# Attention edge gathers of a graph network: lanes without an edge get an index past the table and are left unfetched

## The reference, cut to what matters

```
xn = layernorm(x)
k, q, v = typed_matmul(xn, W, node_type)              # [n, 4 heads, 64]
q_att = einsum('nhd,rhde->rnhe', q, relation_att)     # 8 relations
v_msg = einsum('nhd,rhde->rnhe', v, relation_msg)
score = sum(q_att[etype, dst] * k[src], -1) * relation_pri[etype] / 8
alpha = softmax of score over the edges of one dst
agg   = segment_sum(alpha * v_msg[etype, src], dst)
```

## Time and profile before

| what | us |
|---|---|
| median of three executions | 8423.68 |
| profiled execution | 8421.28 |
| its span | 8419.7 |
| attention stage, first L996 to last L996 | 908.3 to 3488.3 |
| busy in the whole span: TensorE, VectorE, ScalarE, GpSimd | 5151.1, 4515.7, 3197.1, 3888.6 |
| HBM traffic | 878.85 MB read, 280.36 MB written |

### The profile page before, as it was taken

One profiled execution on the slowest core, in us unless ns is written; L12 is line 12 of the kernel. 1 busy time (PEld: TensorE's weight loads), 2 busy tenths in 40 slices (PEclk: granted clock), 3 DMA queues, 4 the chain that ended last, 5 costly groups with the idle time before them and its releaser, 6 DMA issues. The chain is left out here.

```text
span 8419.7 us, 105906 instructions
## 1 busy us (share of the span) xinstructions
PE 5151.1 (61%) x30143; PEld 3822.5 (45%) x30143; DVE 4515.7 (54%) x8736; ACT 3197.1 (38%) x7600; POOL 3888.6 (46%) x3841
## 2 busy tenths in 40 slices
PE   2999566666666666564823333333333257699999
PEld 2555355554555545343712222221222146588888
DVE  5555577777777777634423333343333499833333
ACT  0554466666666666412300100000101067543333
POOL 1221566666666666451267667667776423100000
PEclk7999899999999999886856666655555589799999
DMA  6554777777777777642222222233333468700000
GB/s 142 203 211 191 216 212 214 212 215 213 215 215 210 214 212 213 162 143 93 88 69 66 68 61 66 65 81 83 82 83 82 88 223 287 232 19 12 12 12 12
DMA packets 540060, 1157.67 MB, mean 137 GB/s; under 512 B 121739, under 2 KB 273458, under 8 KB 532798
## 3 DMA queue, kind: packets, MB, share of 16 engines
q0 software_dynamic: 217216, 691.51, 29.0%
q1 hardware_dynamic: 299864, 438.79, 16.2%
q10 hardware_dynamic: 22480, 21.44, 0.8%
HBM read 878.85 MB, written 280.36 MB: 138 GB/s over the span
## 5 line engine op out<-in xcount | busy, mean ns | idle before, releaser
L954 POOL DMA_INDIRECT ae_kv<-edge_table,ae_index x1664 | 1604.5, 964 | 1028.4 <-issue 833.9
L2220 POOL DMA_INDIRECT g_row<-y_parts,g_index x1664 | 1699.1, 1021 | 739.9 <-issue 658.3
L1172 PE MATMUL psum<-ae_kv,ae_edge_hot 128*128 128x266 f32 x3328 | 897.5, 416 | 543.1 <-ACT ae_step_sums L1062 212.7
L1172 PEld LDWEIGHTS psum<-ae_kv,ae_edge_hot 128*128 128x128 f32 x3328 | 629.5, 199 | 797.2 <-issue 407.8
L2241 PE MATMUL psum<-g_row,g_keep 128*128 128x64 bf16 x4992 | 345.4, 216 | 904.0 <-issue 837.1
L1141 PE MATMUL psum<-ae_q,ae_node_hot 128*128 x3328 | 800.8, 395 | 66.2 <-DMA ae_q<-queries 50.0
L996 DVE TENSOR_TENSOR ae_kv<-ae_kv,psum 128x2048 f32<-128x2048 f32 x208 | 475.6, 2287 | 529.2 <-remote 491.0
L2241 PEld LDWEIGHTS psum<-g_row,g_keep 128*128 128x128 bf16 x4992 | 258.7, 113 | 1004.3 <-issue 947.2
L1141 PEld LDWEIGHTS psum<-ae_q,ae_node_hot 128*128 128x128 f32 x3328 | 634.8, 196 | 170.5 <-issue 84.5
L3131 ACT ACTIVATE em_h<-psum,experts_affine 128x256 f32<-128x256 f32 (+1 forms) x800 | 404.4, 555 | 611.7 <-PE psum L3088 432.4
L2414 DVE TENSOR_TENSOR g_acc<-g_acc,g_step_sums 128x64 f32 x832 | 188.3, 226 | 815.8 <-issue 427.1
(11 more groups left out here) (593 smaller groups left out, 10321.5 us busy)
## 6 DMA issues: line engine op xcount, KB each, us to landing
ae_node_hot<-rel_rows SPq DMA_DIRECT2D x208, 512.0 KB
edge_hots<-g_keep SPq DMA_DIRECT2D x208, 356.0 KB
gn_hots<-edge_hots SPq DMA_DIRECT2D x208, 356.0 KB
gn_row<-source_places SPq DMA_DIRECT2D x208, 256.0 KB
ae_kv<-edge_table,ae_index POOLq DMA_INDIRECT x1664
g_row<-y_parts,g_index POOLq DMA_INDIRECT x1664
pair_sums<-gn_out SPq DMA_DIRECT2D x624, 4.0 KB
x_sorted<-nt_x SPq DMA_DIRECT2D x52, 128.0 KB
```

Source lines behind the costliest of these rows:

```text
L954: g.indirect_dma_start(out=kv[:, s, n, :], out_offset=None, in_=dram["table"], in_offset=bass.IndirectOffsetOnAxis(ap=index[:, s, n:n + 1] ...
L1172: ins = t.matmul(bank[4 + m % 2][:, 0:CW], ohs[:, n, :], kv[:, s, n, KC:2 * D], start=n % 2 == 0, stop=n % 2 == 1)
L2220: g.indirect_dma_start(out=row[:, m, n, :], out_offset=None, in_=table, in_offset=bass.IndirectOffsetOnAxis(ap=index[:, m, n:n + 1].bitcas ...
```

## The change

In the index stage VectorE makes a tile `far`: 0 where the destination is below N and inside the block, and FAR = 1,048,576 elsewhere. It sets the first lane of every step and all lanes of the first 64 steps back to 0 and adds `far` to the row of table indices. So an index is either a real one (0 to 49,999) or over a million. In the attention stage each gather takes a bound, R*N - 1 = 49,999, past which a lane is not fetched and no error is raised; that lane keeps what its slot held.

```diff
+        far = sbt("far", [P, RB, P])
...
+            ch.link(v.scalar_tensor_tensor(far[:], st[:, :, 0, :], float(N), inb[:], ALU.is_lt, ALU.mult))
+            ch.link(v.tensor_scalar(far[:], far[:], -float(FAR), float(FAR), ALU.mult, ALU.add))
+            ch.link(v.memset(far[:, :, 0:1], 0.0))
+            ch.link(v.memset(far[0:64, 0, :], 0.0))
+            ch.settle()
+            ch.done(v.tensor_tensor(st[:, :, 2, :], st[:, :, 2, :], far[:], ALU.add))
...
-                                     in_offset=bass.IndirectOffsetOnAxis(ap=index[:, s, n:n + 1].bitcast(U32), axis=0)
-                                     ).then_inc(gathered[s], 16)
+                                     in_offset=bass.IndirectOffsetOnAxis(ap=index[:, s, n:n + 1].bitcast(U32), axis=0),
+                                     bounds_check=R * N - 1, oob_is_err=False).then_inc(gathered[s], 16)
```

## The result

| comparison | before, us | changed, us | ratio, 95% interval |
|---|---|---|---|
| first measurement | 8418.60 (8401.67 to 8434.99) | 8442.72 (8421.99 to 8455.14) | 1.0024 [1.0013, 1.0034] |
| a second one | 8417.21 | 8431.45 (8418.64 to 8442.12) | 1.0018 [1.0009, 1.0027] |
| a third, on another chip | 7728.35 (7726.48 to 7732.76) | 7779.37 (7770.87 to 7785.61) | 1.0063 [1.0049, 1.0077] |

The change makes the kernel slower: by 24 and 14 us where the kernel before takes 8420 us, and by 51 us on a chip where it takes 7728. That one unchanged program takes 9% longer on one chip than on another was not foreseen, and it turned out to decide what the change costs.

A forecast was written before the change was run, and what follows sets the result against it. The prediction took a chain of VectorE and TensorE waits, not gathers, as the bound. 8421.28 + 5.2 (index stage) + 0 (bound) - 1 (lanes left out) = 8425.5 us profiled, median 8428, range 8405 to 8446; likeliest no telling difference, 73%.

The forecast's parts named there:

- Index stage: Five added VectorE instructions ahead of `inblock`, covered by nothing: 5.2 us more, between 4.95 and 6.0.
- So 0.01 to 0.04 us more for each; I take 0.04: Attention stage: extra time the bound adds to each of 1664 gathers, sized from bounded scatters; 0.32 us a group.
- Covered by the 2.46 us that GpSimd waits. Cost 0: Attention stage: the bound's 0.32 us a group hides in GpSimd's wait; cover gone at 0.28 us more a gather.
- L996's idle total down by 50 us or more (the gathers paced it): Profile sign that the forecast is wrong: VectorE's wait before L996 shrinks from 529 us, the gathers having paced it.
- I take -1: Attention stage: 12,891 unfetched lanes, 26.4 MB, shorten nothing on the chain; gain 1 us, bounds 0 and -44.
- VectorE's 9.4 us, then TensorE's 2.8 us: Attention stage: the chain that sets the 12.25 us turn, with the gathers lying beside it.
- The gathers do pace the stage: Rival, attention stage: L996 waits for gathered data, so less traffic gives 8303 to 8357, say 8340 us; 6%.
- Relief of the other transfers: Rival, attention stage: irregular turns come from traffic and give back half of their 44 us: 8407 us; 8%.
- The bounded gather is slow, and GpSimd becomes the bound: Rival, attention stage: from 0.28 us more a gather GpSimd's issues set the turn; at 0.45, 8705 us; 7%.
- The lanes are fetched all the same: Rival, attention-stage gathers: left-out lanes are still fetched or cost as much; 8429 us; 4%.
- A gather reports its end late or not at all: Rival, attention stage: a gather with lanes left out leaves VectorE waiting for `gathered`; under 1%.
- shift by turn-length pattern: Attention stage: a small delay changes how often other turn lengths occur, shifting 20 or more us either way; 4%.

The follow-up runs named there:

- index work only: The changed kernel with `far` all zero and no bound on the gathers: 8421.77 us, ratio 1.0007 to the kernel before.
- bound only: The kernel before with only the bound added to L954's gathers: 8440.38 us, ratio 1.0029; on a quick chip 7791.32 us, ratio 1.0082.
- nothing left out: The changed kernel with `far` all zero, index work and bound kept: 8443.47 us, ratio 1.0034 to the kernel before.
- first-lane run: The changed kernel with `far` at FAR everywhere, so past the first 64 steps each gather fetches one row: 7795.16 us against 7734.87, ratio 1.0077.

## Why the prediction was right, and where it was not

The time, 8442.72, lies in the range, 3 us from its upper end, but the case called likeliest, no difference that can be told, did not come: +24 us (0.24%) is slightly more than that bound. Part of the hit is luck. The sum has 0 for the bound, which alone costs 23 us, and -1 for the lanes left out, which give back about 12; the two errors have opposite signs and partly cancel. The upper end was drawn for the memset and for scatter, not for the bound. And on a chip of the quick kind the same change costs 51 us, for the reason that the sum had ruled out.

**Index stage: right.** Worked out 5.2 us, seen 5.27, and alone +4.6 in the time. The memset of 64x128 took 0.17 us where 0.2 was taken.

**"So 0.01 to 0.04 us more for each; I take 0.04": a little low.** The median rose by 0.052 us, or 0.055 with all lanes fetched (1001 ns), and the mean by 0.06. The trace of before had bounded operations only as scatters, and the nearest rows gave the size to within a few hundredths of a microsecond.

**"Covered by the 2.46 us that GpSimd waits. Cost 0": this step failed.** Alone the bound costs 23 us on the slow kind and 63 on the quick. On the quick kind the reason is shown: there is no cover, GpSimd's issues are the turn, and the threshold of 0.28 us for a gather is 0. The trace of before could not tell that, since on its chip the pause was real. On the slow kind the pause is still there after the change (1.92 to 2.00 us before the first gather of a group), GpSimd is not the bound, and yet 23 us go. What the runs show is that the bound breaks the steady rhythm of 12.25 us: 31 turns near it are left of 146. How the short and long turns come to sum to 23 us is open. The stages of single traces scatter too much (2590.6 us for index work only, 2592.2 for bound only, 2594.7 with nothing left out, 2582.5 and 2577.9 for the changed kernel), and so does what follows the stage (4930.3, 4952.8, 4923.9, 4931.6 and 4933.2 us in the same order). A rival was not tested: all four traces with the bound on this kind have TensorE's granted clock in the stage at 0.91, both without it at 0.96, and TensorE is busy some 90 us longer in it. Against it stands the changed kernel's 2577.9 us at 0.91, which is no longer than the 2580.0 at 0.96. On the quick kind the clock is 0.99 with and without the bound, so there it plays no part.

**The sign "L996's idle total down by 50 us or more (the gathers paced it)": misread.** It is down by 139 us, and the gathers do not pace the stage on this kind: the stage is no shorter, since the idle time moved to L990 and L1023, as shown above. An idle total ahead of one instruction is a sign only together with the length of the turn. Of what was to be seen if the forecast is right, the bytes (26.35 MB fewer), the median gather (998 ns) and the shift of the attention stage (5.2 us) came, and the steady turn of 12.25 us did not. "A number of long turns that differs by several", a sign of being wrong, came: 33 to 69.

**Lanes left out, "I take -1": mis-sized.** 12 us on the slow kind and 17 on the quick. The argument that the gathers are not awaited held for the groups with a few lanes left out. It was wrong to set the last three groups aside as being only three: their lanes all read one row, and such a gather is slow. That they share a row could be read in the code; that a packet takes 306 ns there against 159 needed the run. On the slow kind the last three turns sum to 39 to 41 us with all lanes fetched under the bound and to 35 to 37 with the lanes left out, which would be some 4 of the 12. But the two traces without the bound, in which all lanes are fetched, have 36.9 and 37.4 there, so on that kind even the 4 are not sure, and the rest is open.

**The chain: half of it.** "VectorE's 9.4 us, then TensorE's 2.8 us" describes the slow kind, but the 2.8 us are not work that L996 needs. The matmuls that feed the product at 2511.36 are these, of the kernel before:

```profile
2503.50 3.72 PE L1141 MATMUL psum<-ae_q,ae_node_hot 128*128 x16
```

They end at 2507.22 us by the record, and VectorE is free from 2508.54 on, yet the semaphore increment of the last of them is recorded at 2511.27 and L996 starts at 2511.36. Over the stage this increment comes a median of 4.0 us after that matmul's end, over 0.8 us late in 186 of the 197 turns in which it can be told, and about half a microsecond after the eighth L1172 of the turn has ended. The ends of matmuls are modelled in these traces, but the records of L1150 and L1172, which stand behind L1141 in TensorE's order, begin before the increment. VectorE really waits for it: of the 178 times that L996 follows idle time, it starts within 0.15 us after this increment in 177. On the quick kind the increment comes 0.01 us after the end in every turn. There VectorE's 9.4 us and the gathers' 10.2 are what is left. So L996's "remote" is a late report of TensorE's work, not data, as forecast; "not data" was right, "TensorE's work of the turn" was not.

Why reports are late on one chip and not on another, no run shows. Theory A1, that they hang on GpSimd's gathers, was never tried on the slow kind, but the traces at hand speak for it in two ways. First, the time at which the late report comes. With no bound, half of them come 1.56 to 1.60 us after the recorded end of a gather, nearly always the group's eighth. With the bound alone they come after the sixth, seventh or eighth (36, 44 and 46 of 128), half of them 0.89 to 1.05 us after its end, while the time since the last L1172's end spreads over 0.15 to 0.97. The delay itself falls to a median of 2.9 us and spreads. Second, the place of the 694 us by which the kernel before takes longer on the slow kind (spans 8419.7 and 7725.5 us):

| part of the kernel before | slow kind, us | quick kind, us |
|---|---|---|
| up to the first L996 | 908.3 | 904.6 |
| first to last L996 (gathers L954) | 2580.0 | 2125.0 |
| on to the first gather of the last edge stage (L2220) | 745.7 | 709.6 |
| first to last L2220 | 2431.0 | 2231.9 |
| from there to the end, no gather by GpSimd | 1754.6 | 1754.4 |

Nearly all of it, 654 us, lies in the two stages in which GpSimd issues 1664 gathers one after another, and none in the last 1754 us, though the DMA share is 0.88 from 6800 to 7200 us. So the slow kind is slow beside GpSimd's gathers, and not beside DMA traffic as such. That is a correlation in one pair of traces and no proof; the run that takes gathers away on the slow kind is missing.

**The rivals.** *The gathers do pace the stage* (by traffic) fell with the first-lane run on the quick kind; on the slow kind the stage of the changed kernel is no shorter with 26.35 MB less. Where a gather's data do end the wait, the view says "DMA" and not "remote". *Relief of the other transfers* did not come: long turns went from 33 to 69 instead of becoming fewer. *The bounded gather is slow, and GpSimd becomes the bound* had the right mechanism: it is what happens on the quick kind, but at 0.04 us a gather and not at 0.3, because the pause it counted on is missing there. *The lanes are fetched all the same* fell with the 26.35 MB. *A gather reports its end late or not at all* fell too: with nearly all lanes left out (first lane only) no turn takes over 13.5 us, and the last three take 10.5 to 10.6. The *shift by turn-length pattern*, 4% for both signs, is the nearest to what the slow kind did.

## What to carry to other kernels

A pause that covers an added cost is a property of the run, not only of the program: look at which report ends it (on the slow kind a pause of 1.96 us, ended by a late report, was still there, and yet 23 us went), and price the edit also for the case that the pause is gone. A fixed cost on every issue (here 52 ns x 1664) needs a gain in most of them; here, on the quick kind, 11 of the stage's 15 us of gain sat in three groups, so the next thing to try is a bound on the last groups alone, which no run did. And where padding is fetched, look at which address it goes to: here three groups whose lanes nearly all read one row took about twice as long for each packet as the others.

## What the runs showed of the hardware that was not expected

- The same program took 8417 to 8419 us in two groups of runs and 7728 to 7738 in three others. Of the 694 us between two traces, 455 lie in the attention stage and 199 in the last edge stage, the two in which GpSimd gathers without end, with single instructions equally long (L996 2287 and 2289 ns, L954 946 ns). The last 1754 us, without gathers, are equally long.
- On the slow kind the semaphore increment of TensorE's L1141 comes a median of 4.0 us behind the matmul, about 1.6 us after the end of GpSimd's last gather of the group; on the quick kind it comes after 0.01 us.
- A bound makes a gather 52 ns longer (946 to 998) and adds a MOVE of 29 ns, whether one lane of 128 is fetched or all (998 and 998 ns on the quick kind).
- Where nearly all 1024 lanes of a group fetch one 2 KB row, a packet of the gather queue takes a median of 306 ns against 159, and the core moves 158 GB/s at a DMA share of 0.80. The shared row as the reason is read from the code.
- GpSimd idles 0.30 us between two gathers, and a memset of 0.12 us fits into it for nothing (7737.77 us against 7734.87).
